# Four taps' remainders on GpSimd in every group, three images' statistics on ScalarE, and one queue for two blocks' shuffle

## The chip, the cores and the metric

The kernel runs on one core of a Trainium2 chip. The metric is device time in microseconds (us) of one execution. Engines: TensorE (PE, its weight loads PEld), VectorE (DVE), ScalarE (ACT), GpSimd (POOL), and SyncE (SP), which here only issues DMAs.

## What is computed

The input x is 16 images of 128 channels, 32x32. Two residual layers follow each other (cut to what matters):

```python
def _L0_conv_ref(x, p1, p3, p4, p5, p6):
    t1 = einsum('nchw,he->ncew', x, p1)
    t2 = stack([pad_rows(x)[:, :, k:k + h, :] for k in range(3)], axis=2)
    t3 = depthwise_conv_9x9(t1, p3)
    t4 = conv_5x1(t3, p4, groups=c // 4)
    t5 = einsum('ncew,ewf->ncf', t4, p5[:, :, 0, :])
    t6 = depthwise_conv_1x3(t5, p6)
    return einsum('ncf,nfp->ncp', t6, t2.reshape(n, 3 * c, h * w)) / sqrt(3 * c)

def _L1_conv_ref(x, conv_w, gamma, beta):
    enhanced = concatenate([x, up(cH), up(cV), up(cD)], axis=1)   # Haar details of x, upsampled
    y = einsum('bchw,oc->bohw', enhanced, conv_w)
    return relu(batch_norm(y) * gamma + beta)

x = x + _L0_conv_ref(_gn(x), p1, p3, p4, p5, p6)
x = x + _L1_conv_ref(_gn(x), conv_w, gamma, beta)
```

`_gn` is a group normalization over 4 channels and all pixels of an image. All of it is float32.

## The kernel before, in words

Each product in float32 is made as three faster ones: a value is split into a rounded part ("hi", float32r) and its remainder ("lo" = value - hi), and hi*hi + hi*lo + lo*hi is summed (`split_product`). The making of the lo parts, a subtraction of two SBUF operands in most cases, is a large part of the elementwise work.

The stages in order:

1. Load (0 to 43 us). SP and ScalarE's queue load the 16 images into `x_slot`. VectorE transposes each into `xa` (L853), TensorE multiplies by p1 (`t1_product`), ScalarE copies the result twice, as hi and in full (`t1_high`, L504), GpSimd makes the remainder (`t1_low`, L394).
2. Convolution (43 to 126 us). A loop over 32 groups g of 4 channels. TensorE makes 15 matmuls for the 9x9 convolution (L704 to L721: five taps by three split parts; the last five want `s_lo`), then `t4_product(g - 1)`. The weights of a group, `s_f` (five taps of 128 columns and p4's 128 columns), arrive by DMA in a ring of six (`load_taps`), issued by SP when the remainders of group g - 6 are made (`taps_split`). In iteration g ScalarE copies the group's sum to `t3_hi` (L558), evacuates t4 of group g - 1 (L543), rounds the weights of group g + 2 (`split_high`, L516) and does what is written out by hand for that group: statistics (`ACT_STATS`), parts of p5 (`P5_AT`), `w_det` (`W_DET_AT`), casts of `d_split` (`D_HI_AT`, L551). VectorE in iteration g makes `t3_lo` (L879), its part of the weights' remainder (`split_low(g + 2)`, L859), two statistics halves in groups below 9 and one after (L840), their aggregation (`AGGR_AT`), the group normalization's numbers (`ST1_AT`, `GST_AT`), `p5_lo` in groups 9 to 12 (L911) and remainders of `d_split` (`D_LO_AT`, `d_low`, L868). GpSimd makes the remainder of the first four taps (512 of 768 columns, `taps_low`, L411) in groups 0 to 13; in groups 14 to 31 VectorE makes all 768.
3. Shuffle. t4's output is moved between partitions by DMAs inside SBUF, `d_sb` <- `t_out` (L302), 16 blocks for each of four batches of groups (b = 0 to 3: groups 0 to 8, 9 to 17, 18 to 26, 27 to 31). The blocks of a batch are shared between SP (8, 8, 8, 7) and GpSimd (the rest). SP issues batches 0 and 1 two blocks a step, in the steps g = 18 to 21 and 27 to 30 of its loop over `load_taps(g)`, in which it waits for the remainders of group g - 6. GpSimd issues batch 0's beside taps 10 to 13, batch 1's and 2's after them, and in between the power operation of the group normalization (L437), `w_forms` (six small operations, L414) and two casts (`d_high`, L404). Whoever reads a batch waits for all of it (`wait_d`).
4. p5 product (t5), from 126 us: needs all of `d_split`.
5. A loop over the 16 images (141 to 308 us): output product, second normalization, 1x1 products; then the batch normalization and the stores (308 to 336 us).

The statistics of an image are made by VectorE (two `bn_stats` halves) or by ScalarE (`x_moment`, L518, two passes with accumulators); before, image 0 by ScalarE in groups 2 and 5 (`BY_ACT = 1`), the others by VectorE.

Of the kernel before, what the change touches and what calls it, by code (L numbers as in the profile page):

```python
# [21 lines left out]
F32 = mybir.dt.float32  # L22
# [48 lines left out]
def build(nc, x, p1_blk_in, taps_in, p5_in, p6, w_in, gamma, beta, out):  # L71
    ctx = ExitStack()
    with ctx:
# [239 lines left out]
        def _(sp):  # L313
# [17 lines left out]
            def shuffle_step(step):  # L331

                for b in range(NB - 2):
# [3 lines left out]
                    if 0 <= i < SP_BLOCKS:  # L337
# [14 lines left out]
            shuffle(sp, NB - 2, blocks[:SP_BLOCKS], d_in[NB - 2])  # L352
# [18 lines left out]
        def _(pool):  # L371
# [746 lines left out]
```

## Time and profile before

| | us |
|---|---|
| runs, median of 3 | 339.46 (338.56 to 340.72) |
| profiled execution, its own time | 337.9 |
| its span, first to last instruction | 336.1 |
| busy: TensorE, VectorE, ScalarE, GpSimd | 274.3, 277.9, 231.4, 207.2 |

By the page's chain of waits, the chain that ended last lies 54% of the span on TensorE, 18% on VectorE, 8% on ScalarE, 6% on GpSimd and 5% in DMAs.

In a row of an engine's order of time stand the start in us from the span's start, the duration (of several together where xN is above 1), the engine, the line, the operation with output <- inputs and their shapes, and in brackets the idle time before it with what ended it. Durations are from issue to end and may overlap a little. SPq is SP's queue; DMA_DIRECT2D there is the issuing of a DMA, not its transfer.

### The profile page before, as it was taken

Reading aid. Unit: us, or ns where it says so; the run is one execution under the profiler, and the core shown is the slowest. Engines: PE = TensorE matmul, PEld = TensorE weight load, DVE = VectorE, ACT = ScalarE, POOL = GpSimd, SP = SyncE. Lnnn points to the kernel's source line nnn. Section 1 sums busy time; section 2 is a strip of 40 time slices with the busy share of each in tenths; the row PEclk is TensorE's granted clock in tenths of the full one; section 3 lists DMA queues with packets and bytes.
Section 4 is the critical chain, followed back from the end, with each engine's and each line's share of the span. In section 5 each row is a group of like instructions: output and inputs, shape, how many; then the busy total and the mean of one; then the engine's idle time right before and its main releaser. Section 6 shows DMA issues by size and latency. Waiting matters only on the chain.

```text
span 336.1 us, 4816 instructions
## 1 busy us (share of the span) xinstructions
PE 274.3 (82%) x1544; PEld 226.7 (67%) x1544; DVE 277.9 (83%) x541; ACT 231.4 (69%) x353; POOL 207.2 (62%) x203
## 2 busy tenths in 40 slices
PE   3576599979899889999999999999999998871000
PEld 0111189979799885878888998988889997750000
DVE  3899878997779697768789999999999999765992
ACT  0797838855787657547657778787777787464990
POOL 7398866790029915215878888888898888642000
PEclk9978969998999999999999999999999999987555
DMA  8999456577668376792000000000000000000599
GB/s 216 313 319 277 160 194 184 186 206 208 194 197 245 83 231 168 277 412 102 2 0 3 0 1 2 0 0 2 0 4 1 0 2 0 0 0 1 234 405 360
DMA packets 15096, 43.59 MB, mean 130 GB/s; under 512 B 3056, under 2 KB 3280, under 8 KB 15072
## 3 DMA queue, kind: packets, MB, share of 16 engines
q1 hardware_dynamic: 12672, 36.83, 33.2%
q10 hardware_dynamic: 1344, 4.20, 4.3%
q0 software_dynamic: 1056, 2.27, 2.3%
q8 instruction: 12, 0.20, 0.2%
q14 instruction: 12, 0.10, 0.1%
HBM read 30.44 MB, written 8.39 MB: 116 GB/s over the span
## 4 chain that ended last, share of the span: by engine, by line
PE 54%; DVE 18%; ACT 8%; POOL 6%; DMA 5%; issue 5%; SPq 1%; DVEq 0%; POOLq 0%; ACTq 0%
PE wide L718 10%; PE wide L247 9%; PE wide L249 8%; PE wide L248 8%; DVE xa L853 5%; DVE x_sb L1066 5%; PE bank L795 4%; PE bank L247 4%; PE bank L249 3%; PE bank L248 3%; DMA x_slot<-in_x 3%; DMA d_sb<-t_out 2%; PE bank L799 2%; DVE s_lo L859 2%; DVE d_split L868 2%
## 5 line engine op out<-in xcount | busy, mean ns | idle before, releaser
L718 PE MATMUL wide<-t_all,s_hi 128*128 128x272 f32 (+1 forms) x320 | 47.5, 297 | 2.2 <-ACT t_all L507 1.4
L718 PEld LDWEIGHTS wide<-t_all,s_hi 128*128 128x128 f32 x320 | 43.9, 202 | 3.5 <-ACT t_all L507 2.3
L475 POOL TENSOR_TENSOR g_lo<-y_sb,g_hi 128x1024 fp32r<-128x1024 f32 x15 | 36.1, 2409 | 14.5 <-ACT y_sb L645 14.5
L451 POOL TENSOR_TENSOR g_lo<-y_sb,g_hi 128x1024 fp32r<-128x1024 f32 x15 | 36.0, 2399 | 12.1 <-ACT g_hi L605 12.1
L247 PE MATMUL wide<-g_hi,t_hi 128*128 128x512 f32 x96 | 37.5, 390 | 0.3 <-DVE t_lo L985 0.3
L249 PE MATMUL wide<-g_hi,t_lo 128*128 128x512 f32 x96 | 37.6, 392 | 0.0
L248 PE MATMUL wide<-g_lo,t_hi 128*128 128x512 f32 x96 | 37.4, 390 | 0.0
L853 DVE STREAM_TRANSPOSE xa<-x_slot 128x1024 f32<-128x1024 f32 x16 | 31.3, 2023 | 6.9 <-DMA x_slot<-in_x 6.2
L644 ACT ACTIVATE g_hi<-x_sb,rs 128x1024 fp32r<-128x1024 f32 x16 | 21.3, 1330 | 19.9 <-POOL rs L460 19.9
L859 DVE TENSOR_TENSOR s_lo<-s_f,s_hi 128x768 fp32r<-128x768 f32 (+1 forms) x32 | 25.5, 796 | 9.9 <-ACT s_hi L516 9.7
L302 POOL DMA_DIRECT2D d_sb<-t_out x33 | 16.6, 508 | 26.3 <-ACT t_out L543 26.1
L397 POOL TENSOR_TENSOR t_all<-t_f,t_all 128x512 fp32r<-128x512 f32 x17 | 26.0, 1556 | 8.8 <-ACT t_f L510 8.7
L686 PE MATMUL bank<-xa,p_blk 128*64 128x512 f32 x64 | 21.2, 754 | 10.5 <-DVE xa L853 7.9
L516 ACT CAST s_hi<-s_f 128x768 fp32r<-128x768 f32 x32 | 26.7, 834 | 0.0
L958 DVE TENSOR_TENSOR x_sb<-x_sb,wide 128x512 f32<-128x512 f32 x32 | 21.7, 678 | 5.8 <-PE wide L249 5.8
L558 ACT CAST t_hi<-wide 128x272 fp32r<-128x272 f32 x32 | 12.6, 393 | 19.5 <-PE wide L718 19.5
L718 PE MATMUL wide<-t_all,s_lo 128*128 128x272 f32 (+1 forms) x160 | 25.6, 291 | 0.1
L247 PE MATMUL bank<-p_hi,d_split 128*128 128x384 f32 x68 | 24.6, 362 | 0.7 <-DVE d_split L868 0.7
L411 POOL TENSOR_TENSOR s_lo<-s_f,s_hi 128x512 fp32r<-128x512 f32 x14 | 20.4, 1459 | 7.9 <-ACT s_hi L516 7.8
L686 PEld LDWEIGHTS bank<-xa,p_blk 128*64 128x64 f32 x64 | 3.8, 154 | 28.5 <-DVE xa L853 28.0
L249 PE MATMUL bank<-p_hi,d_split 128*128 128x384 f32 x68 | 23.0, 338 | 0.0
L248 PE MATMUL bank<-p_lo,d_split 128*128 128x384 f32 x68 | 22.9, 337 | 0.0
(136 smaller groups left out, 833.7 us busy)
## 6 DMA issues: line engine op xcount, KB each, us to landing
s_f<-in_taps SPq DMA_DIRECT2D x32, 384.0 KB, 4.0
x_sb<-in_x SPq DMA_DIRECT2D x8, 1024.0 KB, 8.0
out<-x_sb SPq DMA_DIRECT2D x7, 1024.0 KB, 5.1
x_slot<-in_x ACTq DMA_DIRECT2D x12, 256.0 KB, 13.5
x_slot<-in_x SPq DMA_DIRECT2D x12, 256.0 KB, 14.1
d_sb<-t_out POOLq DMA_DIRECT2D x24, 76.5 KB, 3.3
d_sb<-t_out SPq DMA_DIRECT2D x24, 76.5 KB, 3.2
x_slot<-in_x ACTq DMA_DIRECT2D x8, 128.0 KB, 4.6
```

The costliest lines, as they stand in the source:

```text
L247: nc.tensor.matmul(ps, w[0], m[0], start=start, stop=False)
L248: nc.tensor.matmul(ps, w[0], m[1], start=False, stop=False)
L249: return nc.tensor.matmul(ps, w[1], m[0], start=False, stop=stop)
L397: pool.tensor_tensor(t1[:, :, 1, 2:2 + J, at].rearrange("p g j -> p j g"), t1_f[i % 2][:, :, :], t1[:, :, 0, 2:2 + J, at].bitcast(F32).rea ...
L451: pool.tensor_tensor(g1_lo[:, W:W + HW], y_sb[:, n, :], g1_hi[:, W:W + HW].bitcast(F32), ALU.subtract).then_inc(s["g1_lo"], 1)
L475: pool.tensor_tensor(g2_lo[:, :], y_sb[:, n, :], g2_hi[:, :].bitcast(F32), ALU.subtract).then_inc(s["g2_lo"], 1)
L516: act.copy(s_hi[:, g % SR, :], s_f[:, g % WR, :]).then_inc(s["s_hi"], 1)
L686: mm = pe.matmul(ps_t1[i % 4][64 * v:64 * v + 64, :], p1_blk[:, :], rhs, start=True, stop=True)
L718: mm = pe.matmul(ps_t3[g % 2][:, j0 * NO:j1 * NO], weights[:, g % SR, 128 * t:128 * t + 128], t1_all[:, row + j0:row + j1, :].rearrange("p ...
L853: dve.transpose(xa[:, n % 2], x_slot[n // 2][:, n % 2, :].rearrange("p (h w) -> p w h", w=W)).then_inc(s["xa"], 1)
L859: dve.tensor_tensor(s_lo[:, g % SR, first:], s_f[:, g % WR, first:], s_hi[:, g % SR, first:].bitcast(F32), ALU.subtract).then_inc(s["s_lo" ...
L958: dve.tensor_tensor(x_sb[:, n, sl], x_sb[:, n, sl], ps_o[:, sl], ALU.add).then_inc(s["x1"], 1)
```

## The change

- GpSimd makes the remainder of four taps in all 32 groups (`LO_POOL` goes), VectorE always only the last 256 columns.
- ScalarE makes the statistics of images 0 and 1 in the load phase, after its products 6 and 11 (`ACT_STATS_A`), into a bank that the convolution uses later, and those of image 2 in groups 2 and 5. TensorE waits for the first two before the convolution. VectorE has 13 images instead of 15, and no statistics in groups 9 to 12.
- Batches 0 and 1 of the shuffle are issued by SP alone, four blocks a step; GpSimd issues only its parts of batches 2 and 3, after its last taps.
- GpSimd's other work gets places between the taps: `w_forms` after group 23, casts after 27 and 29, the power operation after 30. Aggregation and normalization numbers move by four groups, `w_raw` and `w_det` by three.
- p5's remainder stays in groups 9 to 12, as before.

```diff
-BY_ACT = 1
-ACT_STATS = {2: (0, 0), 5: (0, 1)}
+BY_ACT = 3
+ACT_STATS_A = {6: 0, 11: 1}
+ACT_STATS = {2: (2, 0), 5: (2, 1)}
 EARLY = 8
-LO_POOL, LO_COLS = 14, 4 * C
-AGGR_AT, ST1_AT, GST_AT = 13, 17, 20
+LO_COLS = 4 * C
+AGGR_AT, ST1_AT, GST_AT = 17, 21, 24
...
-W_RAW_AT, W_DET_AT = 21, 16
+W_RAW_AT, W_DET_AT = 24, 19
 SHUFFLE_AT = (18, 27)
-SHUFFLE_POOL_AT = 10
-PER_STEP = 2
-SP_BLOCKS, LAST_SP = 8, 7
+PER_STEP = 4
+SP_BLOCKS, LAST_SP = (16, 16, 8), 7
+POW_AT, W_FORMS_AT = 30, 23
...
-D_HI_POOL = ((1, 2), (1, 3))
-D_LO_AT = {16: (0, 0), 19: (0, 1), 21: (0, 2), 23: (0, 3), 26: (1, 0), 27: (1, 2), 29: (1, 1), 30: (1, 3)}
+D_HI_POOL_AT = {27: (1, 2), 29: (1, 3)}
+D_HI_POOL = list(D_HI_POOL_AT.values())
+D_LO_AT = {16: (0, 0), 19: (0, 1), 21: (0, 2), 23: (0, 3), 26: (1, 0), 28: (1, 2), 29: (1, 1), 30: (1, 3)}
...
-            def two_blocks(b, i):
-                shuffle(pool, b, blocks[SP_BLOCKS + 2 * i:SP_BLOCKS + 2 * i + 2], d_in_pool[b])
-
-            for g in range(LO_POOL):
+            for g in range(G):
                 taps_low(g)
-                if g == SHUFFLE_POOL_AT:
-                    d_ready(pool, 0)
-                if g >= SHUFFLE_POOL_AT:
-                    two_blocks(0, g - SHUFFLE_POOL_AT)
-            d_ready(pool, 1)
-            for i in range(2):
-                two_blocks(1, i)
-            pool.wait_ge(s["gst"], 1)
-            pool.tensor_tensor(rs1[:, 1, :], rs1[:, 0, :], minus_half[:, :].broadcast_to([128, N]),
-                               ALU.pow).then_inc(s["gst_q"], 1)
-            for i in range(2, 4):
-                two_blocks(1, i)
-            w_forms()
-            for b, co in D_HI_POOL:
-                d_high(b, co)
-            d_ready(pool, 2)
-            shuffle(pool, 2, blocks[SP_BLOCKS:], d_in_pool[2])
-            d_ready(pool, 3)
-            shuffle(pool, 3, blocks[LAST_SP:], d_in_pool[3])
+                if g in D_HI_POOL_AT:
+                    d_high(*D_HI_POOL_AT[g])
+                if g == W_FORMS_AT:
+                    w_forms()
+                if g == POW_AT:
+                    pool.wait_ge(s["gst"], 1)
+                    pool.tensor_tensor(rs1[:, 1, :], rs1[:, 0, :], minus_half[:, :].broadcast_to([128, N]),
+                                       ALU.pow).then_inc(s["gst_q"], 1)
+            d_ready(pool, NB - 2)
+            shuffle(pool, NB - 2, blocks[SP_BLOCKS[NB - 2]:], d_in_pool[NB - 2])
+            d_ready(pool, NB - 1)
+            shuffle(pool, NB - 1, blocks[LAST_SP:], d_in_pool[NB - 1])
...
                 t1_high(i)
+                if i in ACT_STATS_A:
+                    for k in range(2):
+                        x_moment(ACT_STATS_A[i], k, wide[0][:, :])
...
                 if g == GB:
-                    act.wait_ge(s["act_stats"], 2)
-                    act.wait_ge(s["x_used"], 2)
+                    act.wait_ge(s["act_stats"], 4)
...
+            pe.wait_ge(s["act_stats"], 2 * len(ACT_STATS_A))
             for g in range(G):
                 pe.wait_ge(s["s_hi"], g + 1)
...
             def split_low(g):
-                first = LO_COLS if g < LO_POOL else 0
                 dve.wait_ge(s["s_hi"], g + 1)
-                dve.tensor_tensor(s_lo[:, g % SR, first:], s_f[:, g % WR, first:],
-                                  s_hi[:, g % SR, first:].bitcast(F32), ALU.subtract).then_inc(s["s_lo"], 1)
+                dve.tensor_tensor(s_lo[:, g % SR, LO_COLS:], s_f[:, g % WR, LO_COLS:],
+                                  s_hi[:, g % SR, LO_COLS:].bitcast(F32), ALU.subtract).then_inc(s["s_lo"], 1)
```

## Rows read from the trace of the kernel before

**Rows 1.** Windows, core 0: us of the stretch and its length, then each engine's busy time
```profile
66.00:76.00 10.00, 8.08 (x59) 7.52 (x58) 9.77 (x14) 5.72 (x12) 8.92 (x12) 0.95 0.77 218
```

**Rows 2.** ScalarE in order of time: start, us, line, instruction, [idle before <- releaser]
```profile
73.23 0.39 ACT L558 CAST t_hi<-wide 128x272 fp32r<-128x272 f32 x1 [0.87 <-PE wide L718]
...
79.08 0.39 ACT L558 CAST t_hi<-wide 128x272 fp32r<-128x272 f32 x1 [1.85 <-PE wide L718]
...
83.47 0.39 ACT L558 CAST t_hi<-wide 128x272 fp32r<-128x272 f32 x1 [0.70 <-PE wide L718]
...
85.72 1.30 ACT L551 CAST d_split<-d_sb 128x612 fp32r<-128x612 f32 x1 [0.75 <-DMA d_sb<-t_out]
86.82 0.42 ACT L558 CAST t_hi<-wide 128x272 fp32r<-128x272 f32 x1
...
111.36 1.31 ACT L551 CAST d_split<-d_sb 128x612 fp32r<-128x612 f32 x1 [1.10 <-DMA d_sb<-t_out]
112.46 0.44 ACT L558 CAST t_hi<-wide 128x272 fp32r<-128x272 f32 x1
...
123.80 0.39 ACT L558 CAST t_hi<-wide 128x272 fp32r<-128x272 f32 x1 [1.40 <-PE wide L718]
...
132.58 2.69 ACT L551 CAST d_split<-d_sb 128x340 fp32r<-128x340 f32 x4 [1.96 <-DMA d_sb<-t_out]
```

**Rows 3.** TensorE in order of time, groups 9 to 12
```profile
65.26 0.76 PE L718 MATMUL wide<-t_all,s_lo 128*128 128x272 f32 x5
...
75.05 0.58 PE L247 MATMUL wide<-t_hi,s_hi 128*128 128x272 f32 x1 [1.85 <-DVE t_lo L879]
...
75.87 2.40 PE L718 MATMUL wide<-t_all,s_hi 128*128 128x272 f32 x10
```

**Rows 4.** VectorE in order of time, groups 8 to 14
```profile
63.21 0.42 DVE L859 TENSOR_TENSOR s_lo<-s_f,s_hi 128x256 fp32r<-128x256 f32 x1
...
68.54 1.60 DVE L911 TENSOR_TENSOR p_lo<-p_raw,p_hi 128x384 fp32r<-128x384 f32 x1
...
75.85 0.54 DVE L911 TENSOR_TENSOR p_lo<-p_raw,p_hi 128x384 fp32r<-128x384 f32 x1
...
80.61 0.96 DVE L859 TENSOR_TENSOR s_lo<-s_f,s_hi 128x768 fp32r<-128x768 f32 x1 [0.67 <-ACT s_hi L516]
```

**Rows 5.** GpSimd in order of time, groups 8 to 31
```profile
63.26 1.53 POOL L411 TENSOR_TENSOR s_lo<-s_f,s_hi 128x512 fp32r<-128x512 f32 x1 [0.48 <-ACT s_hi L516]
...
68.42 1.30 POOL L411 TENSOR_TENSOR s_lo<-s_f,s_hi 128x512 fp32r<-128x512 f32 x1
...
100.65 2.95 POOL L437 TENSOR_TENSOR rs<-rs,minus_half 128x16 f32<-128x16 f32 x1 [6.00 <-DVE rs L905]
...
105.61 1.16 POOL L417 TENSOR_TENSOR w_f<-w_det 128x128 f32<-128x128 f32 x1
...
109.55 0.46 POOL L420 TENSOR_TENSOR w_f<-w_det,w_f 128x128 f32<-128x128 f32 x1
...
126.57 4.39 POOL L302 DMA_DIRECT2D d_sb<-t_out  x9 [7.84 <-ACT t_out L543]
```

**Rows 6.** ScalarE in order of time: a load-phase product, a statistics pass
```profile
24.17 1.14 ACT L507 CAST t_all<-bank 128x512 fp32r<-128x512 f32 x1 [0.47 <-PE bank L686]
...
52.16 1.06 ACT L527 ACTIVATE xa<-x_slot 128x1024 f32<-128x1024 f32 x1
```

**Rows 7.** The tile d_sb: issues, casts, landing (durations min/median/max)
```profile
L302 SPq DMA_DIRECT2D d_sb<-t_out x31: 507/590/1503, 72.7 to 130.0; - x31
L868 DVE TENSOR_TENSOR d_split<-d_sb,d_split x16: 778/1335/1677, 89.5 to 135.5; 128x612 fp32r<-128x612 f32 x12, 128x340 fp32r<-128x340 f32 x4
...
L407 POOL CAST d_split<-d_sb x2: 1268/1279/1290, 111.6 to 112.8; 128x612 fp32r<-128x612 f32 x2
...
DMA to landing us min/median/max: 1.8/3.0/5.9
```

**Rows 8.** SP's queue in order of time, step 21
```profile
81.98 1.49 SPq L302 DMA_DIRECT2D d_sb<-t_out  x2
```

More of the change, by code:

```diff
@@ L270, in taps_split @@
             eng.wait_ge(s["s_lo"], g + 1)
-            eng.wait_ge(s["s_lo_pool"], min(g + 1, LO_POOL))
+            eng.wait_ge(s["s_lo_pool"], g + 1)
         block = ctx.enter_context(nc.Block())
@@ L293, in wait_d @@
         def wait_d(eng, b):
-            by_pool = len(blocks) - (SP_BLOCKS if b < NB - 1 else LAST_SP)
+            by_pool = len(blocks) - (SP_BLOCKS[b] if b < NB - 1 else LAST_SP)
             eng.wait_ge(d_in[b], 16 * (len(blocks) - by_pool))
-            eng.wait_ge(d_in_pool[b], 16 * by_pool)
+            if by_pool:
+                eng.wait_ge(d_in_pool[b], 16 * by_pool)
         def shuffle(eng, b, some, done):
@@ L336, in shuffle_step @@
                         d_ready(sp, b)
-                    if 0 <= i < SP_BLOCKS:
+                    if 0 <= i < SP_BLOCKS[b]:
                         shuffle(sp, b, blocks[i:i + PER_STEP], d_in[b])
@@ L351, in _ @@
             d_ready(sp, NB - 2)
-            shuffle(sp, NB - 2, blocks[:SP_BLOCKS], d_in[NB - 2])
+            shuffle(sp, NB - 2, blocks[:SP_BLOCKS[NB - 2]], d_in[NB - 2])
             sp.wait_ge(s["d_lo"], CI)
@@ L522, in x_moment @@
                     act.wait_ge(x_in[n // 2], 16 * CI)
-                    if n == 0:
-                        act.wait_ge(x_in_first, 16 * CI)
+                    if n in (0, 2):
+                        act.wait_ge(x_in_third if n else x_in_first, 16 * CI)
                 if n or k:
```

## The prediction

> **What bounds the kernel now.** The first view to read is the busy time by stretch. The convolution over 32 channel groups runs from 42.5 to about 125 us; in 66 to 76 us VectorE is busy 9.77 of 10 us while TensorE is busy 8.08 [rows 1]. The second view is ScalarE's order of time: its copy of a group's sum into t3_hi starts when TensorE has finished that group, so the start for group g, called T(g) here, is the pulse of the stage. T(13) = 79.08 and T(15) = 83.47 give 2.19 us a group with nothing in the way. T(12) to T(13) is 5.85 us, 3.7 too long; T(15) to T(16) is 3.35, 1.2 too long; and from T(13) to T(31) the 18 groups take 44.72 us where 39.4 would do, 5.3 too much in all [rows 2]. So TensorE's own work bounds the stage, and about 9 us of it are waits. TensorE's order of time names the wait near 75 us: 1.85 us for VectorE's t3_lo, and then ten matmuls that took 2.40 us at a lower clock [rows 3].
>
> Why VectorE was late stands in its own rows beside GpSimd's. The same p5_lo subtraction takes 1.60 us at 68.54 and 0.54 us at 75.85 [rows 4]; at 68.42 GpSimd's subtraction of four taps runs 1.30 us [rows 5], so VectorE's ran behind it. It goes the other way too: taps at 63.26 take 1.53 us on GpSimd with VectorE's s_lo (0.42 us) begun 0.05 us earlier, and of the six w_forms operations the first takes 1.16 us, beside a VectorE subtraction, and the fourth 0.46 us alone [rows 4, 5]. I read: two-input SBUF operations of the two engines exclude each other.
>
> The Trainium skill ("SBUF — State Buffer", section "SBUF: two separate sides") calls the pair of ports that the two engines share an exclusive lock that whoever starts first holds for the whole instruction. This trace agrees (1.60 against 0.54 us). It speaks against giving GpSimd taps in every group; if the pair were split by bandwidth instead, the two lock terms below would shrink from 2.0 to about 0.5 us.
>
> **The change part by part.**
> (a) Statistics of images 0 and 1 on ScalarE during the load. Each pass took 1.06 us [rows 6], so a pair with its accumulator reads costs about 2.3 us, twice. ScalarE had caught up by its ninth product, where it sat idle 0.47 us for TensorE [rows 6]. Five products follow the second pair; at that much idle each they pay back 2.3 us. Ends: 0 and +2.3; I take +0.3. VectorE loses four statistics halves, in groups 9 to 12.
>
> (b) Groups 9 to 13. GpSimd's eight DMA issues and the statistics leave; p5_lo stays. A group then costs the shared pair about 0.42 + 0.54 + 1.30 = 2.3 us, less small overlaps, against 2.19. The 3.7 us stall goes, and with it the cold clock behind it: -3.7 (ends -4.3 and -2.5). Then T(15) would be 80.1.
>
> (c) What is late next: block 0 of d_sb. ScalarE needs all 16 blocks for d_high in group 15, where it sat idle 0.75 us for them and began at 85.72 = T(15) + 2.25 [rows 2], so it wants them at T(15) + 1.5 = 81.6. SP now issues four a step instead of two, GpSimd none. An issue takes 0.59 us on SP and lands after 3.0 us in the median, 5.9 at worst [rows 7]; before, SP's last two began at 81.98 [rows 8]. A step is then about 0.4 us for the taps and 4 x 0.59 = 2.75 us, longer than a group. The first starts when group 12's remainder is split, about 3.1 us after T(10) = 69.1 (GpSimd's end at 64.79 against T(7), two groups before the end of TensorE's pass at 65.26 + 0.76 [rows 3, 5]): 72.2. Four steps end at 83.2, the last issue begins at 82.6, lands at 85.6; the cast adds 1.1 (85.72 to 86.82). T(16) = 86.7 against 86.82. So +3.3 of the 3.4 gained are given back (ends +2.3 and +6).
>
> The Trainium skill ("DMA: Bandwidth & Descriptors", section "Rules for kernel authors") says that spreading DMAs over issuing engines gains no bandwidth and only saves issue time; here it is issue time that SP lacks, so by that page too the merged queue has nothing to give.
>
> (d) Groups 16 to 22. VectorE's s_lo falls from 0.96 to 0.42 us [rows 4], but GpSimd now holds the shared pair for 1.30 us just when d_low (1.34 us in the median, 1.68 at most [rows 7]) wants it. In a group with d_low the chain t3_lo, s_lo, GpSimd's taps, d_low is 0.4 + 0.4 + 1.3 + 1.3 = 3.4 us, where before it was 0.4 + 1.0 + 1.3 = 2.7. Part of this runs over into groups without d_low. The wait of TensorE for the statistics before its small product only moves from group 18 to 22. I take +0.5 (ends -3, if VectorE's waits vanish, and +3).
>
> (e) w_forms after GpSimd's taps of group 23. Before, they ran from 105.61 to the casts at 111.6, 6.0 us, with no taps behind them [rows 5, 7]. Alone they would be 6 x 0.46 = 2.8 us. Now taps_low(24) is queued behind them; TensorE waits for it, and so does SP, whose step 30 waits for it before the last blocks of block 1. GpSimd has a margin of 2.19 - 1.53 = 0.7 us a group, and its result was ready at 64.79, 0.5 before TensorE's pass over s_lo at 65.26 [rows 3, 5]. The loss lies between 2.8 - 1.2 = 1.6 and 6.0 - 1.2 = 4.8; half behind the lock, I take +2.4.
>
> (f) Block 1, the same as (c), in group 25. Before, ScalarE began that cast at 111.36 [rows 2]. With +2.8 so far (0.3 - 3.7 + 3.3 + 0.5 + 2.4) T(24) is some 108.7; step 30 starts 0.6 us before, its fourth block is issued at about 110.3 and lands 3.0 to 5.9 us later. At 4 us and the 1.1 us cast T(26) is 115.4 against 112.46: +0.1 on top (ends -1.0 and +2.0).
>
> (g) The last groups. GpSimd now does in order, for groups 27 to 31, five taps (7.65 us), two casts of 1.28 us [rows 7] and the power operation, 2.95 us at 100.65 beside VectorE's work [rows 5], bounded by 0.5 and 2.95: 10.7 to 13.2 us against 5 x 2.19 = 10.9, with four d_low in the way. I take +1.5 (ends 0 and +3.5).
>
> (h) The end. Blocks 2 and 3 of GpSimd (8 and 9 issues, 0.49 us each [rows 5]) now queue behind taps_low(31), which ends about 0.7 us before T(31). They are issued until T(31) - 0.7 + 3.9 + 4.4 = T(31) + 7.6, and the last lands 1.5 to 2 us later, at 9.2; before, ScalarE's last casts began at 132.58 = T(31) + 8.8 [rows 2]. +0.5 (ends 0 and +2).
>
> Everything from t5 on is unchanged and shifts. Sum: 0.3 - 3.7 + 3.3 + 0.5 + 2.4 + 0.1 + 1.5 + 0.5 = +4.9 us. The profiled execution took 337.9 us (span 336.1), so it would become 342.8; the median of the runs is 339.46, so 344.4 is predicted for the runs.
>
> **The rivals.**
> VectorE's relief decides (faster). If s_lo's shorter share, 0.54 us in each of 18 groups, keeps VectorE always in time, the 4.1 us of waits between T(16) and T(31) go instead of terms (d) and (g). With (c), (e) and (f) at their low ends, +2.3, +1.6 and -0.9: 0.3 - 3.7 + 2.3 - 4.1 + 1.6 - 0.9 + 0.5 = -4.0; with one of them a microsecond short, -3: 336.5 us. It decides where taps, s_lo and d_low of one group fit into 2.19 us of the shared pair. For it: VectorE was behind its time in all the waits near 75 us. Against: 1.3 + 0.4 + 1.3 is 3.0.
>
> GpSimd is not the bound (no change). w_forms slips into idle time at its low end and the power operation costs 0.5 us; (d) and (g) come to 0 and (e) to 1.6 less one: -3.7 + 0.3 + 3.3 + 0.6 - 0.5 = 0: 339.5 us. For it: GpSimd idled 0.5 to 1 us a group in the taps it had. Against: w_forms' 2.8 us are more than any such gap.
>
> Late landings and the clock (much slower). Blocks land 5.9 us after issue in (c) and (f), +2.9 and +1.9 more, of which about half is hidden, and TensorE, idle over 2 us, restarts at the lower clock as at 75.87, +1: 344.4 + 3.5 = 348 us. For it: one transfer did take 5.9. Against: the median is 3.0.
>
> The change doesn't do what it says: the statistics are moved and GpSimd does take the taps by the code, so only the p5 part is nothing new, since it stood in groups 9 to 12 before.
>
> **How the numbers follow.** Forecast 0.42, faster rival 0.16, no change 0.26, much slower 0.16. About 1%, 3.4 us, is what a measurement can tell from no change: faster is below 336.1, slower above 342.9. The faster rival lies close to that bound (0.11 beyond it); the forecast's own range, 341.5 to 347, puts 0.37 above 342.9. So faster 0.12, same 0.34, slower 0.54. The range 336.5 to 348 leaves about a tenth out on either side.
>
> **What would show it.** T(12) to T(13) near 2.2 us, and p5_lo still taking over 1 us in some groups; a ScalarE wait of 3 us or more for d_sb before the first cast, and T(16) within 1 us of 86.8; a wait of TensorE for GpSimd's s_lo in group 24; t5 starting some 5 us later than before. Wrong it is if T(16) comes at 84 or earlier, if no wait for GpSimd's s_lo shows behind w_forms, or if d_low keeps 1.3 us beside GpSimd's taps.

## The result and the profile after

The changed kernel is slower: 350.01 us in the median of four runs (347.58 to 352.29) against 339.01, a ratio of 1.031, 95% interval 1.025 to 1.036. Timed again later, it took 347.92 us (six runs), ratio 1.027 (1.022 to 1.033). The profiled execution took 347.58 us, its span is 345.5 us, 9.4 us longer than before. The direction was forecast, the size was not: 344.4 us was predicted, at most 348.

ScalarE in order of time in the changed kernel, the rows that answer to [rows 2]; L553 is the copy that starts T(g), L546 the casts of d_split:

```profile
48.86 0.39 ACT L553 CAST t_hi<-wide 128x272 fp32r<-128x272 f32 x1 [3.91 <-PE wide L714]
...
75.00 0.39 ACT L553 CAST t_hi<-wide 128x272 fp32r<-128x272 f32 x1 [0.69 <-PE wide L714]
...
77.18 0.39 ACT L553 CAST t_hi<-wide 128x272 fp32r<-128x272 f32 x1 [0.69 <-PE wide L714]
...
81.57 0.39 ACT L553 CAST t_hi<-wide 128x272 fp32r<-128x272 f32 x1 [0.70 <-PE wide L714]
...
88.74 1.22 ACT L546 CAST d_split<-d_sb 128x612 fp32r<-128x612 f32 x1 [5.67 <-DMA d_sb<-t_out]
89.77 0.41 ACT L553 CAST t_hi<-wide 128x272 fp32r<-128x272 f32 x1
...
126.42 0.39 ACT L553 CAST t_hi<-wide 128x272 fp32r<-128x272 f32 x1 [0.40 <-PE wide L714]
...
132.76 0.39 ACT L553 CAST t_hi<-wide 128x272 fp32r<-128x272 f32 x1 [4.80 <-PE wide L714]
...
136.92 7.30 ACT L546 CAST d_split<-d_sb 128x612 fp32r<-128x612 f32 x8 [1.76 <-DMA d_sb<-t_out]
```

T(0) is 48.86 where it was 45.76, the first such copy in the trace of before:

```profile
45.76 0.39 ACT L558 CAST t_hi<-wide 128x272 fp32r<-128x272 f32 x1 [3.92 <-PE wide L718]
```

T(12) = 75.00 and T(13) = 77.18: the 3.7 us stall is gone. At 88.74 the first cast starts after 5.67 us of waiting for d_sb, and T(16) = 89.77 against 86.82. From T(30) = 126.42 to T(31) = 132.76 pass 6.3 us. Put side by side, by the same pulses of both traces (w_hi is ScalarE's cast of the next weights, the first one behind the last casts of d_split):

```
stretch                   before    after   difference   forecast
start to T(0)              45.76    48.86      +3.1        +0.3
T(0) to T(15)              37.71    32.71      -5.0        -3.7
T(15) to T(16)              3.35     8.20      +4.9        +3.3
T(16) to T(22)             14.67    14.67       0.0        +0.5
T(22) to T(25)              6.84     9.41      +2.6        +2.4
T(25) to T(26)              4.13     3.24      -0.9        +0.1
T(26) to T(31)             11.34    15.67      +4.3        +1.5
T(31) to w_hi              11.23    11.23       0.0        +0.5
w_hi to the end           201.07   201.51      +0.4         0
sum                                            +9.4        +4.9
```

Both columns are one execution each. Two more traces of the kernel before, b2 and b3 below, have 79.8 and 79.9 us from T(0) to T(31) where this one has 78.0; most of that lies in T(16) to T(22), 16.2 us there.

What stands behind the large terms. SP's queue in the changed kernel, steps 18 to 21 (x4 are the four blocks of a step; the single rows are the taps between them), for [rows 8]:

```profile
74.21 2.49 SPq L305 DMA_DIRECT2D d_sb<-t_out  x4
76.80 0.53 SPq L287 DMA_DIRECT2D s_f<-in_taps  x1
77.37 2.41 SPq L305 DMA_DIRECT2D d_sb<-t_out  x4
...
82.97 0.97 SPq L287 DMA_DIRECT2D s_f<-in_taps  x1
83.98 2.71 SPq L305 DMA_DIRECT2D d_sb<-t_out  x4
```

A step takes 3.1 to 3.5 us and not 2.75: the taps' issue behind four blocks takes 0.53 and once 0.97 us, a block 0.60 to 0.68. The issuing of the last block ends at 86.7 and the cast begins 2.05 us later.

GpSimd in order of time, for [rows 5]: taps 23, the first two of the six w_forms operations, taps 24 and 25, taps 28 and 29, taps 30, the power operation, taps 31:

```profile
103.84 1.51 POOL L414 TENSOR_TENSOR s_lo<-s_f,s_hi 128x512 fp32r<-128x512 f32 x1 [1.14 <-ACT s_hi L509]
105.32 0.45 POOL L420 TENSOR_TENSOR w_f<-w_det 128x128 f32<-128x128 f32 x1
105.73 1.61 POOL L421 TENSOR_TENSOR w_f<-w_det 128x128 f32<-128x128 f32 x1
...
109.36 2.70 POOL L414 TENSOR_TENSOR s_lo<-s_f,s_hi 128x512 fp32r<-128x512 f32 x2
...
118.62 3.88 POOL L414 TENSOR_TENSOR s_lo<-s_f,s_hi 128x512 fp32r<-128x512 f32 x2 [0.22 <-ACT s_hi L509]
...
123.84 1.39 POOL L414 TENSOR_TENSOR s_lo<-s_f,s_hi 128x512 fp32r<-128x512 f32 x1
125.18 4.10 POOL L435 TENSOR_TENSOR rs<-rs,minus_half 128x16 f32<-128x16 f32 x1
129.27 1.88 POOL L414 TENSOR_TENSOR s_lo<-s_f,s_hi 128x512 fp32r<-128x512 f32 x1
```

TensorE's waits in the same trace, for [rows 3]: t4 of group 16 and the ten matmuls behind it, the statistics' small product of group 22, the passes over s_lo of groups 24 and 31:

```profile
90.71 0.60 PE L249 MATMUL wide<-t_hi,s_hi 128*128 128x272 f32 x1 [4.81 <-DVE t_lo L874]
...
91.56 2.30 PE L714 MATMUL wide<-t_all,s_hi 128*128 128x272 f32 x10
...
105.86 0.41 PE L724 MATMUL bank<-mv,g_from 128*128 128x32 f32 x2 [1.08 <-DVE mv L894]
...
110.77 0.85 PE L714 MATMUL wide<-t_all,s_lo 128*128 128x272 f32 x5 [1.06 <-POOL s_lo L414]
...
131.29 1.43 PE L714 MATMUL wide<-t_all,s_lo 128*128 128x272 f32 x5 [2.55 <-POOL s_lo L414]
```

The 4.81 us are the late block 0 over again: t4 of group 16 needs t3_lo, which VectorE makes from the copy at 89.77. From 90.7 to 93.0 us, behind this wait, TensorE's granted clock is 0.50, the lower level (1.2 GHz), and ten matmuls take 2.30 us instead of 1.37; it is 0.50 again from 131.2 to 132.8, behind the wait for taps 31.

VectorE, for [rows 4]: the last transposes of the load, p5_lo, d_low, a 13-element operation of the statistics, and the two d_low around the start of the power operation:

```profile
36.67 3.93 DVE L849 STREAM_TRANSPOSE xa<-x_slot 128x1024 f32<-128x1024 f32 x2 [1.31 <-DMA x_slot<-in_x]
...
70.31 1.65 DVE L906 TENSOR_TENSOR p_lo<-p_raw,p_hi 128x384 fp32r<-128x384 f32 x1
...
91.57 2.44 DVE L863 TENSOR_TENSOR d_split<-d_sb,d_split 128x612 fp32r<-128x612 f32 x1
...
104.14 1.25 DVE L893 TENSOR_TENSOR rs<-mv 128x13 f32<-128x13 f32 x1
...
124.00 2.48 DVE L863 TENSOR_TENSOR d_split<-d_sb,d_split 128x612 fp32r<-128x612 f32 x1
...
127.09 1.39 DVE L863 TENSOR_TENSOR d_split<-d_sb,d_split 128x612 fp32r<-128x612 f32 x1
```

p5_lo takes 1.65 us beside GpSimd's taps, as at 68.54 before, and no stall follows. d_low takes 2.44 us behind GpSimd's taps of 91.28 to 92.80, and the 13-element product 1.25 us behind those of 103.84 to 105.35. The d_low of 124.00 runs behind taps 30 and ends at about 126.4; the power operation, issued at 125.18, stands behind it. The d_low of 127.09, inside the power operation, takes 1.39 us, near the 1.34 of the median before.

### The profile page after: what moved, and what is told of

Same layout as the page of the kernel before. It is cut to its first block, busy times and chain, and to the rows that moved or that the text cites. A ratio compares the mean times of both kernels' runs of the same rounds, so it can differ in the third digit from the quotient of the medians.

```text
span 345.5 us, 4829 instructions
## 1 busy us (share of the span) xinstructions
PE 275.5 (80%) x1544; PEld 226.6 (66%) x1544; DVE 278.4 (81%) x535; ACT 235.1 (68%) x361; POOL 228.0 (66%) x205
## 4 chain that ended last, share of the span: by engine, by line
PE 58%; POOL 9%; DMA 8%; DVE 8%; ACT 6%; issue 5%; SPq 3%; DVEq 0%; POOLq 0%; ACTq 0%
PE wide L714 11%; PE wide L249 9%; PE wide L251 8%; PE wide L250 8%; DMA x_slot<-in_x 8%; DVE x_sb L1061 5%; PE bank L791 4%; PE bank L249 3%; PE bank L251 3%; PE bank L250 3%; POOL s_lo L414 3%; PE bank L746 3%; SPq L283 2%; PE bank L795 2%; POOL g_lo L468 1%
## 5 line engine op out<-in xcount | busy, mean ns | idle before, releaser
L414 POOL TENSOR_TENSOR s_lo<-s_f,s_hi 128x512 fp32r<-128x512 f32 x32 | 48.8, 1528 | 25.7 <-ACT s_hi L509 25.7
L714 PE MATMUL wide<-t_all,s_hi 128*128 128x272 f32 (+1 forms) x320 | 46.1, 292 | 2.4 <-ACT t_all L500 1.3
L714 PEld LDWEIGHTS wide<-t_all,s_hi 128*128 128x128 f32 x320 | 42.9, 197 | 4.3 <-ACT t_all L500 2.9
L468 POOL TENSOR_TENSOR g_lo<-y_sb,g_hi 128x1024 fp32r<-128x1024 f32 x15 | 36.2, 2410 | 14.4 <-ACT y_sb L640 14.4
L250 PE MATMUL wide<-g_lo,t_hi 128*128 128x512 f32 x96 | 37.4, 390 | 0.0
L681 PE MATMUL bank<-xa,p_blk 128*64 128x512 f32 x64 | 23.0, 806 | 11.3 <-DVE xa L849 11.0
L854 DVE TENSOR_TENSOR s_lo<-s_f,s_hi 128x256 fp32r<-128x256 f32 x32 | 23.9, 747 | 7.4 <-ACT s_hi L509 7.3
L553 ACT CAST t_hi<-wide 128x272 fp32r<-128x272 f32 x32 | 12.6, 393 | 23.5 <-PE wide L714 23.5
L863 DVE TENSOR_TENSOR d_split<-d_sb,d_split 128x612 fp32r<-128x612 f32 (+1 forms) x16 | 23.9, 1546 | 3.8 <-ACT d_split L546 3.7
L714 PEld LDWEIGHTS wide<-t_all,s_lo 128*128 128x128 f32 x160 | 22.4, 197 | 4.7 <-issue 4.7
L249 PE MATMUL bank<-p_hi,d_split 128*128 128x384 f32 x68 | 24.6, 362 | 0.0
L874 DVE TENSOR_TENSOR t_lo<-wide,t_hi 128x272 fp32r<-128x272 f32 x32 | 13.8, 430 | 13.4 <-ACT t_hi L553 13.3
## 6 DMA issues: line engine op xcount, KB each, us to landing
x_slot<-in_x SPq DMA_DIRECT2D x12, 256.0 KB, 16.2
```

What stands on the lines that cost most here:

```text
L249: nc.tensor.matmul(ps, w[0], m[0], start=start, stop=False)
L250: nc.tensor.matmul(ps, w[0], m[1], start=False, stop=False)
L414: pool.tensor_tensor(s_lo[:, g % SR, 0:LO_COLS], s_f[:, g % WR, 0:LO_COLS], s_hi[:, g % SR, 0:LO_COLS].bitcast(F32), ALU.subtract).then_in ...
L468: pool.tensor_tensor(g2_lo[:, :], y_sb[:, n, :], g2_hi[:, :].bitcast(F32), ALU.subtract).then_inc(s["g2_lo"], 1)
L681: mm = pe.matmul(ps_t1[i % 4][64 * v:64 * v + 64, :], p1_blk[:, :], rhs, start=True, stop=True)
L714: mm = pe.matmul(ps_t3[g % 2][:, j0 * NO:j1 * NO], weights[:, g % SR, 128 * t:128 * t + 128], t1_all[:, row + j0:row + j1, :].rearrange("p ...
```

## The experiments

Spans from T(0) on are compared where the load's variation would hide a difference. Ratios are to the kernel before, timed beside.

**e1, the power operation.** It is replaced by a multiplication, so the first normalization's factors are not computed.

```diff
-                                       ALU.pow).then_inc(s["gst_q"], 1)
+                                       ALU.mult).then_inc(s["gst_q"], 1)
```

> The changed kernel, with GpSimd's power operation after taps 30 replaced by a multiplication of the same shape, so the first normalization's factors are not made. Theory (the power operation of 4.1 us stands before taps 31 and TensorE waits for it): group 30 to 31 falls from 6.3 us to under 3, no wait of TensorE for GpSimd's s_lo in group 31, and the span is 3.5 to 5 us shorter than the changed kernel's. Rival (T(31) is late for another reason, or the shuffle of block 2 sets the end anyway): less than 1.5 us shorter.

343.39 us, ratio 1.015 (1.007 to 1.022). T(30) and T(31) on ScalarE, then the multiplication and taps 31 on GpSimd:

```profile
124.49 0.39 ACT L553 CAST t_hi<-wide 128x272 fp32r<-128x272 f32 x1 [0.39 <-PE wide L714]
...
127.46 0.39 ACT L553 CAST t_hi<-wide 128x272 fp32r<-128x272 f32 x1 [1.42 <-PE wide L714]
```

```profile
123.26 1.40 POOL L435 TENSOR_TENSOR rs<-rs,minus_half 128x16 f32<-128x16 f32 x1
124.61 1.28 POOL L414 TENSOR_TENSOR s_lo<-s_f,s_hi 128x512 fp32r<-128x512 f32 x1
```

T(30) to T(31) is 2.97 us instead of 6.34. The operation itself falls from 4.10 to 1.40 us, and the taps behind it from 1.88 to 1.28; TensorE's clock stays at 1.00 there. So the power operation instead of a multiplication costs TensorE 3.4 us, as the theory had it for this group. Of the span's 5.3 us less, 2.7 are an earlier T(0); from T(0) on the execution is 2.6 us shorter, below the 3.5 expected, since T(31) to w_hi grows from 11.2 to 12.0.

Both durations hold some waiting. In e1 a d_low of VectorE's runs until about 124.5 and the multiplication, issued at 123.26, ends at 124.66; so about 1.2 us of its 1.40 are waiting and 0.2 its own, an estimate from these two rows. The power operation was issued at the same point behind the same d_low: 4.10 - 1.2 = 2.9 us are its own. It took 2.95 us in all three traces of the kernel before, and 2.94 and 2.93 in e6 and e7. VectorE's operations don't wait for it: in the trace of before it runs from 100.65 to 103.6, and d_low inside that time took

```profile
101.86 1.42 DVE L868 TENSOR_TENSOR d_split<-d_sb,d_split 128x612 fp32r<-128x612 f32 x1
```

**e2, w_forms behind the last shuffle.**

```diff
-                if g == W_FORMS_AT:
-                    w_forms()
...
             shuffle(pool, NB - 1, blocks[LAST_SP:], d_in_pool[NB - 1])
+            w_forms()
```

> The changed kernel with w_forms behind all of GpSimd's shuffle instead of after taps 23. Theory (w_forms costs what T(22) to T(25) lost against before, 2.6 us): T(22) to T(25) falls from 9.4 to about 7 us, and the run is 2 to 3 us shorter, if w_hi, which now waits for w_forms, doesn't end later than the casts before it. Rival (d_low behind GpSimd's taps holds those groups): under 1 us.

348.99 us, ratio 1.029 (1.023 to 1.035): no gain that can be told from the changed kernel's. ScalarE's cast of group 25 and w_hi:

```profile
116.44 1.32 ACT L545 CAST d_split<-d_sb 128x612 fp32r<-128x612 f32 x1 [1.14 <-DMA d_sb<-t_out]
...
148.96 0.72 ACT L576 CAST w_hi<-w_f 128x640 fp32r<-128x640 f32 x1 [2.22 <-POOL w_f L425]
```

T(22) to T(25) is 7.9 us, 1.5 less, where 7 was expected. But block 1 holds the cast of group 25 until 116.44, with 1.14 us of waiting where it was 0.42, and w_hi then waits 2.22 us for w_forms. The rest of what T(22) to T(25) had lost, 1.1 us, stays in T(22) to T(23): that is TensorE's wait for the statistics, moved there from group 18.

**e3, SP's steps two groups earlier.**

```diff
-SHUFFLE_AT = (18, 27)
+SHUFFLE_AT = (16, 25)
```

> The changed kernel with SP's shuffle steps two groups earlier (16 and 25 instead of 18 and 27). Theory (SP's issuing of 16 blocks comes too late for the cast in group 15): ScalarE's wait of 5.7 us there goes, T(15) to T(16) falls from 8.2 to under 3.5 us, and the span is 4 to 6 us shorter. Rival (the transfers share the DMA engines with the taps, so that earlier issues only make the taps late, or later d_low waits take it up): under 2 us shorter.

345.1 us, ratio 1.018 (1.012 to 1.023). ScalarE's casts of batch 0 and of batch 3, with T(16) behind the first:

```profile
83.42 1.29 ACT L546 CAST d_split<-d_sb 128x612 fp32r<-128x612 f32 x1 [1.34 <-DMA d_sb<-t_out]
84.52 0.42 ACT L553 CAST t_hi<-wide 128x272 fp32r<-128x272 f32 x1
...
138.87 2.70 ACT L546 CAST d_split<-d_sb 128x340 fp32r<-128x340 f32 x4 [3.04 <-DMA d_sb<-t_out]
```

The wait falls from 5.67 to 1.34 us, T(15) to T(16) from 8.2 to 3.9, and T(0) to T(31) from 83.9 to 79.3. T(15) to T(16) was 3.4 before, so 4.3 of the 4.9 us of that stretch were SP's late issuing; under 3.5 was expected. But T(31) to w_hi is 14.8 us and not 11.2: the chain of waits shows why.

```profile
126.12 7.33 POOL d_sb L305 x15
133.44 5.35 DMA d_sb<-t_out
```

One of GpSimd's last two blocks landed 5.35 us after its issue. SP had issued the reload of images 2 and 3, 1 MB, at 132.97, a microsecond before GpSimd's issues ended at 133.9. It is a new wait; e4, e5, e10 and e11 bear on it.

**e4, the statistics back on VectorE.** ScalarE's and TensorE's waits for these statistics go back with them.

```diff
-BY_ACT = 3
-ACT_STATS_A = {6: 0, 11: 1}
-ACT_STATS = {2: (2, 0), 5: (2, 1)}
+BY_ACT = 1
+ACT_STATS_A = {}
+ACT_STATS = {2: (0, 0), 5: (0, 1)}
```

> The changed kernel with the statistics of images 1 and 2 back on VectorE and those of image 0 in groups 2 and 5, none in the load phase. Theory A (the 3.1 us by which group 0 was late are a slower load in that one execution): T(0) varies between executions with the loads and is not tied to the statistics; here it is 45.5 to 49 and the median of the runs moves by less than 1.5 us. Theory B (the statistics in the load phase cost it): T(0) returns to about 45.8 and the runs are 2 to 3 us shorter. In groups 9 to 12 VectorE has a statistics half again beside p5's remainder; if the pair of ports is what is short there, a stall of 1 to 4 us returns.

350.87 us, ratio 1.034 (1.026 to 1.042), with two runs near 349 and two near 353. T(0) is 47.9 without any statistics in the load. T(12) to T(15) is 7.7 us instead of 6.6: the halves beside p5_lo cost 1.1 us. Moving the statistics was good for that much, and cost nothing visible in the load. The median is 0.9 us above the changed kernel's first and 3.0 above its later one; theory A allowed 1.5.

The profiled execution took 352.9 us. T(31) to w_hi is 14.8 us in it instead of 11.2: ScalarE's last casts, and the chain of waits before them:

```profile
146.33 2.68 ACT L547 CAST d_split<-d_sb 128x340 fp32r<-128x340 f32 x4 [2.98 <-DMA d_sb<-t_out]
```

```profile
141.00 5.25 DMA d_sb<-t_out
```

It is e3's late landing: SP issued the reload at 140.66, 0.8 us before GpSimd's issues ended at 141.5. In the changed kernel's first two traces (347.6 and 346.7 us) the reload was issued 0.2 to 0.3 us before that end, and the last casts did not wait.

**b2 and b3, the kernel before, and a2, the changed kernel, looked at again.**

> The kernel before, unchanged, for another profiled execution. Question: how much of the 3.1 us by which group 0 started late in the changed kernel is the load's own variation. Theory A (variation): T(0) comes at 46 to 49 here too, with VectorE's transposes ending at 38 to 40.5 us, and T(0) to T(31) stays 77.5 to 78.5. Theory B (the change delays the load): T(0) stays within 0.5 us of 45.8.

> The kernel before, unchanged, once more, for the same question: by theory A T(0) differs from the other two executions of it by up to 2.5 us, by theory B by under 0.5 us.

> The changed kernel, unchanged, for a second profiled execution. By theory A its load phase varies as that of the kernel before does. The waits named so far repeat: T(15) to T(16) 8 to 9 us, T(22) to T(25) 9 to 10, T(30) to T(31) 6.3. If this execution is one of about 352 us, the last batch's casts start 3 to 4 us later after T(31) than in the first (4.2 and then no wait), with a DMA of GpSimd's landing over 5 us after its issue behind SP's reload.

T(0) of the kernel before came at 47.6 and 47.2, with 45.8 in its first trace; the changed kernel's at 47.1 in a2 and in a3 below, where it had been 48.9. ScalarE's first copy, and VectorE's last transposes with the statistics that end them, of b2:

```profile
47.64 0.39 ACT L558 CAST t_hi<-wide 128x272 fp32r<-128x272 f32 x1 [3.93 <-PE wide L718]
```

```profile
35.26 3.96 DVE L853 STREAM_TRANSPOSE xa<-x_slot 128x1024 f32<-128x1024 f32 x2 [0.48 <-DMA x_slot<-in_x]
39.11 2.46 DVE L840 BATCH_NORM_STATS2 sty<-x_slot 128x6 f32<-128x512 f32 x4
```

The transposes ended at 38.1 in the first trace of before, 39.1 and 39.5 in the other two, and between 38.1 and 40.5 in the changed kernel and its variants. T(0) follows them by 7.6 to 8.5 us in all. So the 3.1 us are the load's own variation: two traces of each kernel have T(0) at 47.1 to 47.6.

T(0) to T(31) was 78.0, 79.8 and 79.9 us before, where theory A had expected 77.5 to 78.5, and 83.9, 84.6 and 85.1 after (a2 and a3 the last two). What b2 and b3 have more is mostly TensorE's clock: 0.64 from 94.5 to 98.0 us in b2 and 0.65 from 94.0 to 97.6 in b3, behind the wait for the statistics in group 18, where the first trace has 1.00 behind the same wait; T(18) to T(19) is 5.6 us and not 4.4. a2 took 346.68 us and showed no late landing.

**e5, e11, e10 and a3, the order of the reload.** e5 and e11 hold it behind GpSimd's blocks, e10 puts it ahead of SP's own, a3 is the changed kernel beside e11 and e10.

e5 and e11:

```diff
             sp.wait_ge(s["d_lo"], 2 * CI)
+            sp.wait_ge(d_in_pool[NB - 1], 16 * (len(blocks) - LAST_SP))
             reload_x(sp, 1)
```

e10:

```diff
-            d_ready(sp, NB - 1)
-            shuffle(sp, NB - 1, blocks[:LAST_SP], d_in[NB - 1])
             sp.wait_ge(s["conv"], G)
             sp.wait_ge(s["d_lo"], 2 * CI)
+            d_ready(sp, NB - 1)
             reload_x(sp, 1)
+            shuffle(sp, NB - 1, blocks[:LAST_SP], d_in[NB - 1])
```

> The changed kernel; SP waits for GpSimd's nine blocks of batch 3 before it issues the reload of images 2 and 3. Theory (a reload of 1 MB that is issued before GpSimd's last blocks overtakes them; this is what makes some runs of the changed kernel 4 to 5 us longer than others, 347.6 and 352.3): the runs lie together near 347 to 348.5 and none above 350, the median is 1 to 3 us under the changed kernel's. Rival (the spread is the load phase's or chance): runs of both sizes remain.

> The changed kernel, unchanged, timed in the same call as the next two. So far its runs were 347.6, 352.3, 347.8, 352.2 and 346.7 us. Theory (the reload overtakes GpSimd's last blocks in some executions): runs of both sizes, a median of 347.5 to 350, and longer runs than e11's by 1.5 us or more in the median. Rival (load and clock alone spread the runs): the same distribution as e11's within 1 us.

> e5_reload_after once more beside the changed kernel: SP waits for GpSimd's nine last blocks before the reload. Theory: median 346 to 347.5, few or no runs above 350. Rival: as the changed kernel.

> The changed kernel with SP's reload of images 2 and 3 (1 MB) issued before SP's seven blocks of batch 3, so always before GpSimd's last blocks too. Theory (a reload ahead of the blocks holds them up): the last casts wait, ScalarE's w_hi comes 13.5 to 15 us after T(31) instead of 11.2, and the median is 2 to 4 us above e11's, near 350 to 351. Rival (blocks and reload share the engines without harm): w_hi stays at 11 to 12 us after T(31).

Medians: e5 347.08, e11 347.27, a3 347.92, e10 351.20 us. The DMA view gives GpSimd's nine last blocks with their median time from issue to landing, first of a3, then of e10:

```profile
d_sb<-t_out POOLq DMA_DIRECT2D x9, 42.5 KB, 1.9
```

```profile
d_sb<-t_out POOLq DMA_DIRECT2D x9, 42.5 KB, 5.2
```

With the reload ahead of them the blocks land 5.2 us after their issue (SP's seven after 5.4, and it is one of those that the chain of waits goes through), w_hi comes 14.4 us after T(31), and all six runs of e10 lie at 350.7 to 352.9. That part is shown. That it is what made two of the changed kernel's first runs take 352 us is likely, by e4's trace of 352.9 us, but no such run of the changed kernel itself has a trace. As a matter of medians the order of the reload is worth little: a3 and e11 differ by 0.6 us, as the rival had it and less than either spreads, and e5 has a run of 350.3 that its theory excluded.

**e6, VectorE's taps from group 14 on.** GpSimd's other work stays where the change put it.

```diff
-LO_COLS = 4 * C
+LO_POOL, LO_COLS = 14, 4 * C
...
-            eng.wait_ge(s["s_lo_pool"], g + 1)
+            eng.wait_ge(s["s_lo_pool"], min(g + 1, LO_POOL))
...
             for g in range(G):
-                taps_low(g)
+                if g < LO_POOL:
+                    taps_low(g)
...
+                first = LO_COLS if g < LO_POOL else 0
-                dve.tensor_tensor(s_lo[:, g % SR, LO_COLS:], s_f[:, g % WR, LO_COLS:],
-                                  s_hi[:, g % SR, LO_COLS:].bitcast(F32), ALU.subtract).then_inc(s["s_lo"], 1)
+                dve.tensor_tensor(s_lo[:, g % SR, first:], s_f[:, g % WR, first:],
+                                  s_hi[:, g % SR, first:].bitcast(F32), ALU.subtract).then_inc(s["s_lo"], 1)
```

> The changed kernel with all 768 columns of the weights' remainder on VectorE from group 14 on, as before the change; GpSimd's other work stays where it stands, but no taps are queued behind it. Theory (w_forms, the power operation and the lock cost through GpSimd's taps): T(16) to T(31) falls from 43 us to 37 to 39, no wait for GpSimd's s_lo is left, and the runs are 5 to 8 us shorter, near 342; the wait of ScalarE in group 15 stays. Rival (VectorE is the bound there and GpSimd relieves it): T(16) to T(31) stays above 42.

343.57 us, ratio 1.012 (1.006 to 1.018). The waits of e6 from 76 to 135 us (engine and line, what for; us in all, times, longest):

```profile
PE wide L249 <- DVE t_lo L876: 9.0, 5, 6.1
ACT d_split L547 <- DMA d_sb<-t_out: 7.9, 2, 6.9
```

TensorE waits for GpSimd's s_lo nowhere; in the changed kernel it did three times, 3.8 us in all. T(16) to T(31) is 37.4 us instead of 43.0. T(16) to T(22) is 14.7 us with GpSimd's taps and without: there VectorE's relief and the lock cancel. The runs are 4.4 us shorter than the changed kernel's later median and 6.4 shorter than its first, where 5 to 8 was expected.

**e8, e3 and e2 together.**

```diff
-SHUFFLE_AT = (18, 27)
+SHUFFLE_AT = (16, 25)
...
-                if g == W_FORMS_AT:
-                    w_forms()
```

(with w_forms behind the last shuffle, as in e2)

> The changed kernel with the earlier shuffle steps of e3 and w_forms behind the last shuffle as in e2. In e2 the 1.5 us gained to T(25) were given back at the cast of group 25, which waited for block 1. Theory (that wait was SP's lateness): with the early steps T(22) to T(26) is 12.1 us in e3 and falls to 9.5 to 10.5 here, and T(0) to T(31) is 1.5 to 2.5 us shorter than e3's 79.3; at the end w_hi waits 2 to 3 us for w_forms, so the run is within 2 us of e3's. Rival (d_low behind the taps holds those groups): T(0) to T(31) within 0.7 us of e3's.

344.62 us, ratio 1.014 (1.009 to 1.019). T(22) to T(25) is 7.9 us as in e2, T(22) to T(26) 11.1, above the expected 9.5 to 10.5, and T(0) to T(31) 78.6 against e3's 79.3: the rival's number. With block 1 no longer late, 1.0 us of w_forms' 1.5 stays gained at T(26), and T(26) to T(31) takes back 0.5 of it. So w_forms is 1.5 of the 2.6 us at T(25), and 1.0 at T(26).

**e7, e6 and e3 together, and e9, with four edits more.** e9 adds to e7:

```diff
-D_HI_AT = {15: (0, 0), 18: (0, 1), 20: (0, 2), 22: (0, 3), 25: (1, 0), 28: (1, 1)}
+D_HI_AT = {16: (0, 0), 18: (0, 1), 20: (0, 2), 22: (0, 3), 25: (1, 0), 28: (1, 1)}
-D_LO_AT = {16: (0, 0), 19: (0, 1), 21: (0, 2), 23: (0, 3), 26: (1, 0), 28: (1, 2), 29: (1, 1), 30: (1, 3)}
+D_LO_AT = {17: (0, 0), 19: (0, 1), 21: (0, 2), 23: (0, 3), 26: (1, 0), 28: (1, 2), 29: (1, 1), 30: (1, 3)}
...
-                if g == ST1_AT + 1:
+                if g == ST1_AT + 2:
...
+            sp.wait_ge(d_in_pool[NB - 1], 16 * (len(blocks) - LAST_SP))
             reload_x(sp, 1)
```

> As e6_taps_vector, and SP's shuffle steps two groups earlier (16 and 25). Theory (what is left of the change, four blocks a step on SP and no GpSimd work beside p5's remainder, gains the 4 to 5 us of groups 9 to 13 once the blocks come in time): T(15) to T(16) under 4 us, and the runs are 3 to 6 us shorter than the kernel before, 333 to 336. Rival (a later wait takes the gain): within 1 per cent of the kernel before.

> e7_vector_early (VectorE's taps from group 14 on, SP's steps at 16 and 25), and the first cast and remainder of batch 0 one group later (16 and 17), the statistics' small matmul one group later, and the reload behind GpSimd's last blocks as in e5. Theory: T(15) to T(17) falls from 5.3 to about 4.4 us, T(22) to T(23) from 3.1 to 2.3, so 1.5 to 2.5 us shorter than e7: a median of 336 to 338, 0.5 to 1 per cent under the kernel before. Rival (what e7 gained in the convolution is lost in something that the runs share, so that these edits too don't show): within 0.5 per cent of the kernel before.

e7 took 338.99 us, ratio 0.997 (0.993 to 1.000); its profiled execution took 335.16, T(0) to T(31) 73.1 us against 78.0 to 79.9 of before. So my 333 to 336 held for that execution and not for the median of twelve runs, 335.2 to 340.8; what spreads them is not known, and by its median e7 can't be told from the kernel before. e9 took 336.33 us, ratio 0.991 (0.988 to 0.994): 0.9% faster than the kernel before, a small difference, but the interval leaves out 1. Its T(0), T(15), T(16), T(31) and w_hi on ScalarE:

```profile
46.97 0.39 ACT L555 CAST t_hi<-wide 128x272 fp32r<-128x272 f32 x1 [3.92 <-PE wide L716]
...
79.71 0.39 ACT L555 CAST t_hi<-wide 128x272 fp32r<-128x272 f32 x1 [0.70 <-PE wide L716]
...
81.89 0.39 ACT L555 CAST t_hi<-wide 128x272 fp32r<-128x272 f32 x1 [0.69 <-PE wide L716]
...
118.23 0.39 ACT L555 CAST t_hi<-wide 128x272 fp32r<-128x272 f32 x1 [1.40 <-PE wide L716]
...
129.60 0.80 ACT L579 CAST w_hi<-w_f 128x640 fp32r<-128x640 f32 x1
```

T(15) to T(16) is 2.2 us, since the cast of block 0 now comes one group later; it finds the block there and waits for nothing. T(15) to T(17) is 4.7 us against e7's 5.3 (4.4 was expected). T(22) to T(23) is 2.5 against 3.1, but T(22) to T(25) is 7.6 against 7.5: the later small product gained nothing by T(25). The four edits were not run one by one.

## Why the prediction was wrong in size

(a) Load: nothing speaks against +0.3. The 3.1 us in the profile are variation between executions; the kernel before alone shows 1.9 us of it (b2, b3), and the changed kernel 1.7.

(b) Groups 9 to 13: the mechanism held. The stall went and p5_lo still ran 1.65 us behind GpSimd's taps. The gain to T(15) was 5.0 us in the first pair of traces, 5.2 between b2, b3 and a2, 4.7 between them and a3, not 3.7: I had counted only T(12) to T(13), and not the 0.6 us before it. The rest of the 5.0 is group 1, which varies with the execution (T(0) to T(1) 2.8 to 3.3 us before, 2.1 to 3.1 after).

(c) Block 0: the mechanism held, the size failed. +3.3 was forecast, +4.9 came, because "about 0.4 us for the taps and 4 x 0.59" was 3.1 to 3.5 us a step, 1.9 us more from the first block to the last, of which an earlier landing gave 0.4 back: the taps' issue took 0.53 to 0.97 us behind four blocks, a block 0.60 to 0.68. e3 shows that 4.3 of the 4.9 were SP's issuing. And the wait reached further than T(16): the clock at 0.50 behind it cost 0.9 us more in the ten matmuls of 91.56, which I had only in the rival "Late landings and the clock".

(d) Groups 16 to 22: +0.5 forecast, 0.0 measured, -1.5 against b2 and b3. It is a sum of more than I had named: the statistics' wait and, in b2 and b3, the low clock behind it left this stretch (T(18) to T(19) was 4.4 and 5.6 us, now 2.7), and the 0.9 us of (c) came in. What the taps themselves did there is e6's 14.7 against 14.7: the longer d_low (2.44 us) and the shorter s_lo cancelled. GpSimd's subtractions and VectorE's excluded each other whole, down to 13 elements that took 1.25 us. That is the exclusive lock of the Trainium skill ("SBUF — State Buffer", section "SBUF: two separate sides"), and this trace agrees for them. It does not for the power operation, during which VectorE's d_low took 1.39 us as if alone: that operation waits for VectorE's but does not hold VectorE's up, and there the measurement decides. The price of the lock depends on slack, and VectorE had some once the weights' share was small.

(e) w_forms: +2.4 forecast, +2.6 measured, but right by luck. The middle of my bounds, 1.6 and 4.8, with half behind the lock, is 3.2 and not 2.4. e2 gives w_forms 1.5 us: it took 4.1 us and not 6.0, with one of its six operations above 1 us where four were. The other 1.1 is TensorE's wait for the statistics in group 22, 1.08 us; I had said that it "only moves", yet booked it in (d).

(f) Block 1: +0.1 forecast (T(24) should have read 106.16 + 2.8 = 109.0 there, so +0.4), -0.9 measured: TensorE's own lateness in group 24 covered SP's. e2 uncovers it: what w_forms gives back, block 1 takes.

(g) The last groups is the step that failed: +1.5 forecast, +4.3 measured (3.5 to 4.3 over all traces of both kernels). I set 10.7 to 13.2 us of GpSimd's work against 10.9, "with four d_low in the way" at no price. Taps 27 to 31 with what stands between them took 15.5 us, 115.6 to 131.1, with 0.2 us of idle time. The lock's waiting behind VectorE made the taps 8.5 us instead of 7.65, the casts 3.1 instead of 2.6, and the power operation 4.10 instead of at most 2.95. I had also misread that 2.95, bounding it down to 0.5 as if it could be waiting, like the w_forms rows: all of it was the operation's own work, and the lock's 1.2 us came on top. e1 gives the power operation, against a multiplication that waits as long, 3.4 us of TensorE's time: 2.7 its own, 0.6 in the taps behind it, which in the changed kernel wait behind one more d_low (128.74 to 130.0). Without it T(26) to T(31) is 12.3 us, 0.6 to 0.9 above before, which is left to the taps and casts. e6 takes the taps away instead and leaves the power operation, and that stretch is 11.3 us, as before: the operation is on TensorE's path only because taps 31 are queued behind it.

(h) The end: +0.5 forecast, 0.0 measured; the last casts followed the earlier ones without a wait.

The "two lock terms" of 2.0 us beside the lock are no two terms of the sum: (d) and what (e) has above its low end are 0.5 + 0.8 = 1.3.

From T(0) to the end the profiled execution grew by 6.3 us where 4.6 was forecast: (g) and (c) came 4.4 us higher, (b), (d), (f) and (h) 3.3 us lower, (e) and the rest of the run 0.6 us higher. By the other traces the growth is 4.8 to 7.9 us, so these terms are good to about 1.5 us in all. The rest of the error is in the measured values: the load adds 2.8 us to that one execution, and the first median, 350.0, stands 2.1 us above the later one of the same kernel. The rival "VectorE's relief decides" fell: e6, which takes the relief back, is faster. So did "GpSimd is not the bound": TensorE waits for its s_lo in groups 24 and 31. "Late landings and the clock" named two real dangers. The late landings were in the wrong place: they are at the last blocks, behind a reload (e3, e4, e10), not in (c) or (f). The clock did fall to 0.50 behind the long waits, and the forecast had no term for it.

## What to carry to other kernels

An engine that runs a short periodic task for the bottleneck has only its period minus that task to spare, here 0.7 us a group. A long operation queued among such tasks goes on the path for what exceeds the idle time ahead of it, however small its share of busy time: w_forms, 4.1 us behind groups with some 1 us of idle time each, cost 1.5; the power operation, 4.1 us behind casts that had used the idle time up, cost 3.4. Price DMA issues by a row with as many issues in a line as the change makes, and start them by when the last must have landed. And look up what ran on the other engine when an operation was issued, before putting a long duration down to waiting or to work: 2.95 us was work, and 1.2 of the 4.10 was waiting.

## What the runs showed that I had not expected

A power operation on 128x16 elements takes GpSimd 2.93 to 2.95 us by itself in five traces, and 4.10 behind a d_low; a multiplication of the same shape some 0.2 (an estimate, 1.40 less the 1.2 it waited). While it runs, VectorE's two-input subtractions take their usual time (1.39 us at 127.09, 1.42 at 101.86), whereas GpSimd's subtraction of four taps holds them up to its end. A DMA's time from issue to landing depends on what another queue issued a fraction of a microsecond earlier: GpSimd's 42.5 KB blocks landed after 1.9 us with the reload issued as their last were, and after 5.2 us with its 1 MB ahead. With the reload 0.8 to 1.0 us ahead of the end of their issuing (e4, e3), a last block took 5.3 us and the casts waited 3.0; with 0.2 to 0.3 us (the changed kernel's first two traces) they didn't wait.
